# Causal attention: the lower query half's products with the values, in one run at a pair's boundary instead of two

## What is computed

```python
q = (x @ Wq).reshape(b, n, HEADS, DIM_HEAD).transpose(0, 2, 1, 3) * scale
kv = jnp.concatenate([null_kv broadcast to (b, 1, DIM_HEAD), x @ Wkv], axis=1)
sim = jnp.where(causal_mask, mask_value, jnp.einsum('bhid,bjd->bhij', q, kv))
out = jnp.einsum('bhij,bjd->bhid', jax.nn.softmax(sim, axis=-1), kv)
return out.transpose(0, 2, 1, 3).reshape(b, n, HEADS * DIM_HEAD) @ Wout
```

## Time and profile before

| what | value |
|---|---|
| median of 3 runs | 1290.66 us (1290.0 to 1292.76) |
| profiled execution, time | 1291.22 us |
| its span, first to last instruction | 1289.5 us |
| TensorE busy over the span | 1173.5 us (91%) |
| VectorE, ScalarE, GpSimd busy | 1063.0, 941.8, 304.1 us (82%, 73%, 24%) |
| from 470 to 900 us of the span: TensorE busy | 417.47 of 430 us, granted clock 1.00 |
| the same stretch: VectorE, ScalarE, GpSimd busy | 302.64, 302.61, 175.18 us |

### The profile page before, as it was taken

How to read it: one execution, slowest core, us unless ns; L and a number is a source line. 1 busy time by engine, 2 the same in 40 slices (tenths; PEclk the granted TensorE clock), 3 DMA queues, 4 the chain that set the end, 5 groups by cost and what they waited for, 6 DMA issues and landing times. The chain is left out here.

```text
span 1289.5 us, 32074 instructions
## 1 busy us (share of the span) xinstructions
PE 1173.5 (91%) x10916; PEld 508.9 (39%) x10916; DVE 1063.0 (82%) x1787; ACT 941.8 (73%) x2001; POOL 304.1 (24%) x534
## 2 busy tenths in 40 slices
PE   4499999999987899999999999998769999999996
PEld 3112222222225655555666556555622222222222
DVE  6889999998987777777755777776589999999896
ACT  3169999998983677777755777775239999998894
POOL 4400000021010344444423444443330000000200
PEclk9679999999996999999999999999869999999998
DMA  4811212354210001000000000000431212245312
GB/s 112 242 27 56 66 48 54 91 87 79 70 34 25 18 18 34 18 18 18 18 18 18 17 18 18 18 18 2 147 99 47 69 46 59 69 79 91 81 45 66
DMA packets 51792, 69.54 MB, mean 54 GB/s; under 512 B 21168, under 2 KB 29296, under 8 KB 51696
## 3 DMA queue, kind: packets, MB, share of 16 engines
q1 hardware_dynamic: 51696, 68.26, 21.7%
HBM read 37.30 MB, written 22.54 MB: 46 GB/s over the span
## 5 line engine op out<-in xcount | busy, mean ns | idle before, releaser
L949 DVE TENSOR_REDUCE neg_max<-ps 128x1 f32<-128x1024 f32 x512 | 591.3, 1215 | 28.3 <-PE ps L1218 26.3
L785 ACT ACTIVATE arena<-ps 128x512 f32<-128x512 f32 x1024 | 545.5, 597 | 88.0 <-PE ps L1233 75.8
L1233 PE MATMUL ps<-arena 50*128 50x512 bf16 x1024 | 324.9, 389 | 16.8 <-ACT arena L785 9.9
L1249 PE MATMUL ps<-arena 128*32 128x256 f32 (+1 forms) x3584 | 317.4, 426 | 8.5 <-ACT arena L785 3.1
L1218 PE MATMUL ps<-arena 48*128 48x512 bf16 x1024 | 298.2, 398 | 15.4 <-DVE neg_max L949 14.4
L1021 DVE TENSOR_REDUCE a_neg_max<-ps 128x1 f32<-128x129 f32 (+7 forms) x256 | 191.8, 749 | 115.3 <-PE ps L1370 114.3
L638 POOL TENSOR_SCALAR arena<-arena,a_rsum 128x128 f32<-128x128 f32 (+7 forms) x256 | 192.0, 750 | 320.8 <-DVE a_rsum L1040 314.4
L721 ACT ACTIVATE arena<-ps,a_neg_max 128x129 f32<-128x129 f32 (+7 forms) x256 | 189.4, 740 | 50.8 <-DVE a_neg_max L1021 38.4
L1365 PE MATMUL ps<-arena 64*128 64x128 f32 (+6 forms) x512 | 192.9, 458 | 0.0
L1363 PE MATMUL ps<-arena 64*128 64x321 f32 (+7 forms) x512 | 188.3, 451 | 4.7 <-DVE neg_s_null L1052 1.9
L1233 PEld LDWEIGHTS ps<-arena 50*128 50x128 bf16 x1024 | 74.0, 94 | 297.2 <-ACT arena L785 266.8
(11 more groups left out here) (130 smaller groups left out, 827.0 us busy)
## 6 DMA issues: line engine op xcount, KB each, us to landing
arena<-stack_dram SPq DMA_DIRECT2D x128, 192.0 KB, 3.4
stack_dram<-arena SPq DMA_DIRECT2D x48, 256.0 KB, 3.6
o_dram<-arena SPq DMA_DIRECT2D x32, 256.0 KB, 2.1
arena<-arena SPq DMA_DIRECT2D x32, 256.0 KB, 3.5
arena<-o_dram SPq DMA_DIRECT2D x30, 256.0 KB, 4.3
arena<-max_dram SPq DMA_DIRECT2D x256, 1.0 KB
x<-in_L_attn_x SPq DMA_DIRECT2D x2, 512.0 KB, 5.2
max_dram<-max_T SPq DMA_DIRECT2D x64, 8.0 KB, 1.7
```

The costliest lines, as they stand in the source:

```text
L785: nc.scalar.activation(probs[:, t, :], ps[:, EXP_BANK[t], :], ACT.Exp, scale=F_SCALE).then_inc(probs_ready, 1)
L949: nc.vector.tensor_reduce(neg_max[:, g, t:t + 1], ps[:, bank:bank + 2, :].rearrange("p a b -> p (a b)"), AX, ALU.max, negate=True).then_in ...
L1233: ins = nc.tensor.matmul(ps[:, bank, :], stack[rows, g, 1, kt * P:(kt + 1) * P], stack[rows, g, 0, h * HALF:(h + 1) * HALF], start=True, s ...
L1249: ins = nc.tensor.matmul(ps[row:row + 32, PV_BANK, cols], v_unit[:, g, t // 2, :], probs[:, t, cols], start=j == 0 and c0 == 0 and g % 2 == 0,
```

## The change

The lower half's values get one part instead of two. `per` becomes 4, so all four key tiles run in the step that had the second part: tile 0 of the next pair. The step of tile 15 has no values any more.

```diff
-        V_STEPS = ((15, 16), (21, 25, 27, 29))
+        V_STEPS = ((16,), (21, 25, 27, 29))
```

## The result

The changed kernel took 1301.99 us (median of 4 executions, 1298.7 to 1302.79) where the kernel before took 1290.33 (4 executions beside it, 1285.92 to 1292.76): a ratio of 1.0087 with a 95% interval of 1.0065 to 1.0108. The forecast was 1299.0 us: 8.3 us on 1290.66, a ratio of 1.0064. The change makes the kernel slower.

The account below looks back on a forecast made before the run. TensorE's own work and the waits its order causes bound the kernel. Thirteen boundaries at 0.48 us (6.2 us), with -0.04, 1.42 and 0.70, gave 8.3 us more: 1299.0 us, range 1291.0 to 1303.1 for eight times in ten.

Parts of the forecast that it names:

- The bound: Attention pairs: TensorE's work and the waits its order causes set the length (27.99 us); later waits make nothing up.
- The saving: Lower half's values at each boundary: one joint run of 2.30 us, one start fewer, saves 0.16 us a pair.
- the prediction's estimate: Joint run's saving taken as two drains of 0.05 us a pair; the sum would be about 0.9 us higher.
- The lost cover: Regular boundary: tile 12's transposes wait for ScalarE's copy of tile 11, 0.77 us later; 0.48 us a boundary net.
- The boundaries that differ: After pair 0, 0.04 us less; after pair 8, 1.42 us more; at the end of pair 15, 0.70 us more.
- The sum: 13 boundaries at 0.48 us are 6.2 us; with -0.04, 1.42 and 0.70 this gives 8.3 us.
- the forecast of the profile: Changed profile: pair of 28.47 us, TensorE's busy time about 0.16 us less, tile 14's transposes still waiting 0.18 us.
- That ScalarE's copy is done in time: Rival at tile 12's transposes: no wait, only the saving counts, 2.6 us faster, about 1288.1 us; chance 0.07.
- That the lateness is made up: Rival inside the pairs: small waits elsewhere shrink and the 0.48 us vanish, about 1291 us; chance 0.11.
- second wait of size: Rival in tiles 1 to 3: joint run starves other engines, about 1.1 us a boundary, 1307 us; chance 0.05.

Follow-up runs that it names:

- e2: Against the kernel before, two parts again: key tile 0 in the step of tile 15, key tiles 1 to 3 in tile 0's step; 1289.98 us, ratio 0.9984.
- e4: Against the changed kernel, matmuls of key tiles 2 and 3 done once more, uselessly, in the step of tile 15; 1300.7 us, ratio 1.0066 to the kernel before.
- e5: Against the changed kernel, tile 11's two copies exchanged between ScalarE and VectorE; 1321.51 us, ratio 1.0234 to the kernel before.
- second comparison: The changed kernel run again without edit, beside the kernel before; 1300.84 us against 1292.1, ratio 1.0066.
- e3: Against the changed kernel, the joint run of all four key tiles put in the step of tile 15; 1293.84 us, ratio 1.0014 to the kernel before.
- e6: Against the kernel before, the second part (key tiles 2 and 3) one step later, in the step of tile 1; 1289.16 us, ratio 0.9986.
- repeated run: The unedited changed kernel run and profiled again, beside the kernel before; 1300.84 us, ratio 1.0066.

## Why the prediction came out as it did

The third point below uses one more row of the kernel before, tile 11's transposes ahead of the first row:

```profile
580.79 0.68 PE L1383 MATMUL ps<-ident,arena 64*128 64x64 f32 x14
```

- **The bound.** Right. Wherever a boundary got longer, the pair got longer by the same amount; no later wait gave any back. The wait of tile 14's transposes is 0.18 us, as in the earlier trace rows, and ScalarE's idle time before the copy of tile 13 is 0.21 us (0.22 in the earlier trace rows): the chain moved along whole.
- **The saving.** Right in size: the joint run takes 583.33 - 581.03 = 2.30 us, as forecast, 0.16 us less than the two runs. On the same line lie the 1.01 us of 512 columns and the 1.45 us of 768 in e2. That these 0.16 us are the change of mode was not tried apart from other costs of starting a run. They are above the 0.11 us of the prediction's estimate, two drains of about 128 cycles by the Trainium skill (TensorE: Matmul & The Clock Gate, Part 2: What happens when you issue a matmul). The times of the whole cannot tell the two apart.
- **The lost cover.** Right: transposes 0.14 us after the copy, 0.45 us for the transposes alone (580.58 to 581.03). TensorE is free at 579.57: that is 0.61 us after the row of tile 11's transposes at 578.96, as in the kernel before from 580.79 to 581.40. From there to tile 1's scores it is 583.33 - 579.57 = 3.76 us, against 3.28: 0.48 us a boundary, the forecast. e4 and e5 show that it is a wait and whose it is. One term was off without harm: tile 0's scores start 0.52 us after TensorE is free (579.57 to 580.09), not 0.44, since they come 0.14 to 0.15 us after the exponential's end at every boundary where they wait, not the 0.06 us read in the earlier trace rows before tile 1's scores. The copy, which opens later, sets the boundary's length all the same.
- **The boundaries that differ.** Pair 0: tile 13's scores to the next pair's tile 1 take 9.97 us (430.56 to 440.53) instead of 10.00 (434.18 to 444.18), 0.04 less forecast. Pair 8: the transposes waited 1.49 us for the output tile's addition; from that addition's start to tile 1 it is 3.14 us (676.66 to 679.80) against 1.75, 1.39 more, 1.42 forecast. The tail: from TensorE's being free to the last run 7.86 us (884.98 + 0.61 = 885.59 to 893.45) against 7.12 (881.54 to 888.66), 0.74 more, 0.70 forecast.
- **The sum.** 8.3 us forecast; 8.5 and 9.2 us in the attention stage of the two profiles, 8.5 us by the ratio of the second comparison. Of the 9.2 us, 0.7 lie in pair 0 ahead of its boundary, where the change has not acted yet: from the first scores to tile 13's it is 29.58 us (402.93 to 432.51) against 28.88 before (405.30 to 434.18). The first comparison's 11.7 us between medians of four executions each is above the forecast, and its 1301.99 us lie 3 us above the 1299.0; its interval reaches down to 8.4 us.
- **What the forecast of the profile had wrong.** TensorE's busy time did not fall by 0.16 us a pair; it is 27.56 us where it was 27.51. The run is shorter, but tile 0's scores and tile 12's transposes no longer run among each other: from the scores to the values it is 0.94 us (580.09 to 581.03) instead of 0.82, and the modelled ends count part of the wait as busy.
- **The rivals.** That ScalarE's copy is done in time was wrong, as the rows had it. That the lateness is made up was wrong. No second wait of size appeared in tiles 1 to 3.

## What to carry to other kernels

Before moving work out of a step, list what the other engines finish while it runs, and who asks for that straight after: here a run of 1.66 us was the time in which ScalarE freed a score place and a bank, and a start cost of 0.16 us saved was paid for with a wait of 0.64. How much cover is needed can be read off as the difference between the time when the next instruction could go and the time when its last gate opens, here 0.77 us, and work of at least that length did (0.81 us in e4, 1.0 us in e2). It has to be taken from a place where it covers nothing itself: e3 and e6 only moved the wait on. A gap can be tested by filling it: if useless work of known length in it moves the time by little, the engine was waiting there.

## What the runs showed that was not expected

Short waits that come close together were in some places followed by a lower clock of TensorE, and then cost more than their sum. In e5 the boundary has two waits, 0.45 us and 0.84 us, within some 2 us. The table of windows around the start of two of e5's pairs (columns as in the earlier trace rows, the granted clock third from the end):

```profile
527.70:529.60 1.90, 1.01 (x18) 0.87 (x18) 1.51 (x5) 1.57 (x3) 0.81 (x2) 1.00 0.00 0
529.60:531.60 2.00, 2.00 (x10) 0.71 (x10) 0.74 (x3) 0.89 (x5) 1.59 (x2) 0.62 0.00 0
531.60:533.60 2.00, 2.00 (x14) 0.92 (x10) 0.00 (x0) 0.00 (x0) 0.21 (x1) 0.52 0.00 0
...
589.90:591.70 1.80, 0.96 (x16) 0.83 (x16) 1.47 (x5) 1.47 (x3) 0.71 (x2) 1.00 0.00 0
591.70:594.10 2.40, 2.40 (x22) 1.12 (x18) 0.75 (x3) 0.94 (x5) 1.85 (x2) 1.00 0.04 10
```

After the same two waits the joint run went at about half the full clock, the 1.2 GHz level, in one pair (4.06 us) and at the full 2.4 GHz in the other (2.37 us). Seven of e5's sixteen boundaries had such a spell, and in each the joint run took 1.4 to 1.7 us longer than 2.37 us, 11.4 us in all: four of the thirteen regular ones, whose pairs are 31.0 to 31.2 us long in place of 29.4, with a mean clock of 0.94 or 0.95, and those after pairs 0 and 8 and in the tail. The attention stage of this profile is 24.1 us longer than in the first profile of the changed kernel; the 12.7 us that the spells leave are about the 12 us expected of the waits. No regular pair of the other seven profiles had a spell. What picks the pairs was not tried. The changed kernel has 0.45 us and a short second wait and kept a clock of 1.00 through its regular pairs, but in the first profile its tail, where TensorE waits four times for 0.67 to 0.93 us, was followed by a lower clock (0.77 granted from 893.45 to 901.00), and the last run of values took 7.51 us (first section). In e3, whose tail also has four such waits (0.64 to 0.79 us), it took 7.29 us. In the repeated run, with the same four waits as in the first, it takes 5.81 us, and so it does in the kernel before and in e4, whose tails have three such waits. So the 1.7 us come and go between executions of the changed kernel, and were no part of the forecast.
